# A post-norm attention and mixture-of-experts layer on eight cores: the softmax bound's broadcast moved behind the first score matmuls

## The reference, cut to what matters

```python
def reference(x, Wq, bq, Wk, bk, Wv, bv, Wo, bo, Wg, W1, W2, W3, bias):
    # x: (4, 2048, 2048); 16 heads of 128; 8 experts, 2 per token, FFN 1024
    q, k, v = proj(Wq, bq), proj(Wk, bk), proj(Wv, bv)
    q, k = apply_rotary(q), apply_rotary(k)
    attn = softmax(q @ k.T * 128 ** -0.5)
    a = (attn @ v) @ Wo.T + bo
    x = layernorm(x + a)
    w = top2(sigmoid(x @ Wg.T) + bias)
    f = sum over e of (silu(x @ W1[e].T) * (x @ W3[e].T) * w[e]) @ W2[e].T
    return layernorm(x + f)
```

## Time and profile before

| | us |
|---|---|
| median of 3 runs | 3051.35 |
| lowest and highest run | 3049.73, 3329.33 |
| the profiled execution | 3052.92 |
| its span (first to last instruction, slowest core, core 6) | 3051.4 |
| spans of the eight cores | 3035.5 to 3051.4 |
| PE busy | 2589.0 |
| DVE busy | 772.0 |
| ACT busy | 593.5 |

### The profile page before, as it was taken

How to read it: one execution, slowest core, us unless ns; L and a number is a source line. 1 busy time by engine, 2 the same in 40 slices (tenths; PEclk the granted TensorE clock), 3 DMA queues, 4 the chain that set the end, 5 groups by cost and what they waited for, 6 DMA issues and landing times.

```text
span 3051.4 us, 31195 instructions; the slowest of 8 cores (3035.5 to 3051.4 us)
## 1 busy us (share of the span) xinstructions
PE 2589.0 (85%) x12262; PEld 1193.6 (39%) x12262; DVE 772.0 (25%) x1140; ACT 593.5 (19%) x761; POOL 172.5 (6%) x323
## 2 busy tenths in 40 slices
PE   4778788888887878799579998999999899998993
PEld 3234343435352525244134343444434344343441
DVE  0222222222213131321632213122221312212126
ACT  0342424242423333342100000000000000000031
POOL 1000000000000000000000001010010100001000
PEclk9889999899898999999589999999999999999996
DMA  9310101010101010024134444443444434344423
GB/s 147 49 28 14 28 14 28 14 28 15 28 14 28 15 28 8 7 36 76 26 51 73 62 79 65 70 76 64 79 65 77 65 67 76 63 76 63 69 45 121
DMA packets 50720, 155.26 MB, mean 51 GB/s; under 512 B 6162, under 2 KB 6290, under 8 KB 49298
## 3 DMA queue, kind: packets, MB, share of 16 engines
q0 software_dynamic: 47264, 142.69, 28.8%
q1 hardware_dynamic: 3314, 10.59, 1.0%
HBM read 287.54 MB, written 8.39 MB: 97 GB/s over the span
## 4 chain that ended last, share of the span: by engine, by line
PE 74%; DMA 9%; DVE 8%; issue 5%; ACT 3%; DVEq 0%; ACTq 0%; POOL 0%; POOLq 0%
PE pb L776 15%; PE pb L793 14%; PE pb L850 9%; DMA wslab<-w_t 7%; PE pb L318 6%; PE pb L395 6%; PE pb L401 6%; PE pb L448 4%; PE pb L468 4%; PE pb L539 4%; PE pb L454 3%; DMA R_bf<-x_t 2%; DVE scr_f L341 1%; ACT scr_bf L361 1%; PE pb L370 1%
## 5 line engine op out<-in xcount | busy, mean ns | idle before, releaser
L850 PE MATMUL pb<-aog,wslab 128*128 128x512 bf16 x2048 | 460.6, 381 | 61.6 <-DMA wslab<-w_t 60.9
L776 PE MATMUL pb<-xy,wslab 128*128 128x512 bf16 x2048 | 464.4, 386 | 0.0
L793 PE MATMUL pb<-xy,wslab 128*128 128x512 bf16 x2048 | 452.5, 379 | 0.0
L787 ACT ACTIVATE scr_bf<-pb 128x512 bf16<-128x512 f32 x128 | 69.5, 594 | 1326.9 <-PE pb L776 1326.9
L850 PEld LDWEIGHTS pb<-aog,wslab 128*128 128x128 bf16 x2048 | 195.3, 98 | 323.4 <-issue 102.8
L476 ACT ACTIVATE scr_bf<-pb,mq_sb 128x1024 bf16<-128x1024 f32 x256 | 285.1, 1114 | 136.0 <-PE pb L468 135.9
L395 PE MATMUL pb<-R_bf,wslab 128*128 128x512 bf16 x768 | 297.4, 387 | 5.8 <-ACT vbuf L306 5.8
L776 PEld LDWEIGHTS pb<-xy,wslab 128*128 128x128 bf16 x2048 | 202.4, 99 | 251.5 <-issue 18.8
L401 PE MATMUL pb<-R_bf,wslab 128*128 128x512 bf16 x768 | 296.4, 386 | 0.0
L793 PEld LDWEIGHTS pb<-xy,wslab 128*128 128x128 bf16 x2048 | 200.3, 98 | 241.7
L863 DVE TENSOR_TENSOR R_f<-pb,R_f 128x512 f32<-128x512 f32 x256 | 177.1, 692 | 347.4 <-PE pb L850 334.1
(11 more groups left out here) (111 smaller groups left out, 1460.6 us busy)
## 6 DMA issues: line engine op xcount, KB each, us to landing
wslab<-w_t POOLq DMA_DIRECT2D x128, 512.0 KB, 5.1
wslab<-w_t POOLq DMA_DIRECT2D x128, 256.0 KB, 3.8
wslab<-wv_t POOLq DMA_DIRECT2D x8, 1024.0 KB, 8.5
R_bf<-x_t POOLq DMA_DIRECT2D x16, 512.0 KB, 7.3
wslab<-wq_t POOLq DMA_DIRECT2D x8, 1024.0 KB, 8.5
wslab<-wk_t POOLq DMA_DIRECT2D x8, 1024.0 KB, 8.0
wslab<-wo_t POOLq DMA_DIRECT2D x16, 512.0 KB, 5.0
y<-R_f SPq DMA_DIRECT2D x16, 512.0 KB, 2.7
```

Of the source, the lines that this page charges most:

```text
L776: last = t.matmul(pa[nc2].ap(), wslab.ap()[:, W1OFF[s1] + dc * 128: W1OFF[s1] + dc * 128 + 128], xy.ap()[:, dc * TL + nc2 * 512: dc * TL + ...
L793: last = t.matmul(pa[4 + nc2].ap(), wslab.ap()[:, W3OFF[s1] + dc * 128: W3OFF[s1] + dc * 128 + 128], xy.ap()[:, dc * TL + nc2 * 512: dc * ...
L850: last = t.matmul(pa[wb + nc2].ap(), wslab.ap()[:, W2OFF[s2] + fc * 128: W2OFF[s2] + fc * 128 + 128], aog.ap()[:, fc * TL + nc2 * 512: fc ...
```

## The change

The broadcast of the bound (the matmul and the write of `mq_sb`) leaves `bound_finale` and becomes a function of its own, `bound_bcast`. It uses bank pa6 in place of pa3. `st_merged` now issues the scores of chunks 0 and 1, then this function, then both exps, then the sums of chunk 0; from chunk 2 on the loop is as it was: scores, exp, sums of the chunk before.

```diff
--- before.py
+++ after.py
@@ -429,18 +429,20 @@
                 A(lambda s: s.activation(msc.ap()[0:1, 7:8], msc.ap()[0:1, 7:8],
                                          AF.Exp, scale=0.5),
                   r=["msc"], w=["msc"])
+
+            def bound_bcast():
                 T(lambda t: t.matmul(
-                    pa[3].ap()[:, 0:1], ones_r_f.ap(), msc.ap()[0:1, 7:8],
-                    start=True, stop=True), r=["msc", "ones"], w=["pa3"])
+                    pa[6].ap()[:, 0:1], ones_r_f.ap(), msc.ap()[0:1, 7:8],
+                    start=True, stop=True), r=["msc", "ones"], w=["pa6"])
                 V(lambda v: v.tensor_scalar(
-                    mq_sb.ap()[:, 6:7], pa[3].ap()[:, 0:1], -1.0, None,
-                    ALU.mult), r=["pa3"], w=["mq"])
+                    mq_sb.ap()[:, 6:7], pa[6].ap()[:, 0:1], -1.0, None,
+                    ALU.mult), r=["pa6"], w=["mq"])
 
             proj_rope(4, 4096 + hl * 2048, ["ws2" if hl == 0 else "ws3"], bkc,
                       "bkc", ck_sb, sk_sb, kbuf, koff,
                       [f"kb{hl}_{i}" for i in range(4)], finale=bound_finale)
 
-            def st_merged():
+            def st_merged(pre=None):
                 def sums_pvs(kc):
                     j = kc % 2
                     so = (1 - j) * 1024
@@ -461,7 +463,7 @@
                             r=[f"sb{2 * (1 - j) + qb}", f"vb{kc}"],
                             w=[f"pa{4 + qb}"])
 
-                for kc in range(NDC):
+                def emit_mms(kc):
                     j = kc % 2
                     for qb in range(2):
                         T(lambda t, kc=kc, j=j, qb=qb, qoff=qoff, koff=koff:
@@ -472,6 +474,9 @@
                             start=True, stop=True),
                             r=[f"kb{hl}_{kc // 4}", f"qb{hl}_{qb}"],
                             w=[f"pa{2 * j + qb}"])
+
+                def emit_exp(kc):
+                    j = kc % 2
                     so = (1 - j) * 1024
                     A(lambda s, j=j, so=so: s.activation(
                         scr_bf.ap()[:, so:so + 1024],
@@ -479,8 +484,18 @@
                         scale=SCALE),
                         r=[f"pa{2 * j}", f"pa{2 * j + 1}", "mq"],
                         w=[f"sb{2 * (1 - j)}", f"sb{2 * (1 - j) + 1}"])
-                    if kc >= 1:
-                        sums_pvs(kc - 1)
+
+                emit_mms(0)
+                emit_mms(1)
+                if pre is not None:
+                    pre()
+                emit_exp(0)
+                emit_exp(1)
+                sums_pvs(0)
+                for kc in range(2, NDC):
+                    emit_mms(kc)
+                    emit_exp(kc)
+                    sums_pvs(kc - 1)
                 sums_pvs(NDC - 1)
 
             def epilogue_m():
@@ -503,7 +518,7 @@
                         AF.Identity, bias=bvc.ap()[:, hh:hh + 1]),
                         r=[f"ao{hh}", "bvc"], w=[f"ao{hh}"])
 
-            st_merged()
+            st_merged(pre=bound_bcast)
             epilogue_m()
 
     for gi in range(NH // 2):
```

## The result

The changed kernel took 3069.62 us (median of 10 runs) against 3049.64 us for the kernel before (median of 10 runs on the same chip): the ratio is 1.0067, with a 95% interval of 1.0056 to 1.0078. It is slower by 20 us, 0.7%. In some executions of both kernels (near 3400 us), and in the profiles of x3, x4 and x11 further down, the cores of a die ran at a lower granted clock than the others, and the ratios and the means over cores leave them out.

The account below looks back on a forecast made before the run. The prediction took PE's matmul stream as the bound. A later first exp (11.2 us) and a later clock return (17.6 us) summed to 28.8 us, giving a forecast of 3080 us, range 3060 to 3096.

Parts of the forecast that it names:

- What bounds the kernel: TensorE's matmul stream, busy 85% of the span; the step from key projection to attention loop comes once in 16 heads.
- What the change removes: On PE, L336 and the scores of chunk 0 no longer stand behind the 2.56 us wait, finishing before anything needs them.
- What it adds: On DVE, mq waits behind L341, L345 and L349, so first exp and sums come 0.70 us later per head: 11.2 us.
- The loop edit: Two score steps issued ahead of the attention loop cost and give nothing, since PE and ACT keep their order.
- The flush on DVE: A flush behind L349 by the skill page, 0.96 us per head, 15 us in all; left out of the sum.
- The clock: PE's clock returns 3.1 us later, 2.4 us more at half clock, at 0.46 per us: 1.1 per head, 17.6 us.
- list of signs: What the new trace would show if right or wrong; mq starting before L349 ends on DVE counted as wrong.
- Sum: Whole kernel: 11.2 + 17.6 = 28.8 us slower, 3080 us, 0.9% more; under 2% not told from no change.
- Shift alone: Rival: PE's clock return moves with the work, so only 11.2 us are added, 3063 us; chance 0.17.
- Not slower: Rival: unbroken PE work ahead of the sums brings the clock back early, -3 us in all, 3048 us; chance 0.08.
- Half clock through the loop: Rival: the pause keeps PE's clock down through the whole attention loop, 264 us more, 3315 us; chance 0.03.
- A deeper prefetch: Rival: the loop keeps scores one chunk further ahead, removing waits before the exps, 72 us less, 2979 us; chance 0.01.

Follow-up runs that it names:

- x3: Changed kernel with mq written ahead of L349 on DVE, not behind it, PE's order unchanged; ratio 1.0066 to the kernel before.
- x4: Changed kernel with 8 unneeded matmuls per head, 3 ahead of the scores of chunk 1, 5 ahead of the sums; ratio 0.9960 to the kernel before, median 3032.16 us.
- x11: Changed kernel with 9 unneeded matmuls in each of two PE pauses between the heads; ratio 1.0038 to the kernel before.
- x6: x4 with 11 in place of 5 matmuls ahead of the sums, and L349 done twice for the last key pair; ratio 1.0048 to the kernel before, 3062.33 us.
- x1: Changed kernel with broadcast and mq write put back in their old place, only the loop edit kept; ratio 1.0020 to the kernel before, median 3050.87 us.
- x2: Changed kernel with mq written between L341 and L345, broadcast ahead of the scores of chunk 1; ratio 0.9920 to the kernel before, median 3016.27 us.
- x7: x2 with 3 unneeded matmuls per head, 2 ahead of the broadcast, 1 ahead of the sums; ratio 0.9873 to the kernel before, median 3010.38 us.
- x8: x7 with 18 more unneeded matmuls per head ahead of the second L370 of the keys; ratio 0.9858 to the kernel before, median 3010.13 us.
- x9: x8 with 9 unneeded matmuls ahead of the first L370 of the query projection and of the first key half; ratio 0.9833 to the kernel before, 3002.56 us.
- x5: Kernel before the change with 5 unneeded matmuls per head between L370 and the broadcast L432; ratio 0.9991 to the kernel before, median 3048.38 us.

## Why the prediction was right, point by point

- *What bounds the kernel* stood. PE's stream is what counts, and the step comes 16 times in the same form.
- *What the change removes*: the wait of L432 is gone and L336 follows L370 at once, and this gained nothing by itself, as said.
- *What it adds*: DVE decides and not PE, as said. The first exp was forecast at 4.28 to 4.44 and measured at 4.20, the sums at 5.67 and measured at 5.57. The term of 0.70 us per head was 0.60: L341 began at 0.36, not at 0.41 or later, since it overlaps the end of L423, as L437 overlaps the end of L349. The first exp came only 0.51 later; the rest of the 0.60 is that the sums now start 1.37 us behind it, where I took the 1.28 of before. That was 9.6 us in place of 11.2. x6 shows, in the filled kernel, that the term is carried to the end in full.
- *The loop edit* does nothing, as said (x1).
- *The flush on DVE*: L437 begins 0.07 us before the recorded end of L349, and the repeated addition in x6 cost 1.31 us for an operation of 1.23. The 0.96 us that an estimate from the Trainium skill ("VectorE: DVE Perf Modes", "The DRAIN you can't avoid") would put behind each isn't there. The prediction told that section in part: it also says that a next operation that is not held starts earlier, and the trace agrees with that. The prediction's own list of signs called it wrong if mq starts before L349 ends; by 0.07 us it does, as the prediction's steps for mq themselves allow, so that sign was badly put.
- *The clock* was the right mechanism and the largest term. Its return was forecast 3.1 us later, 2.4 of them in the loop, at 0.46 us each: 17.6 us. Measured were 2.06 us more in the loop, and 13 us are left for them. So the shift was a little high, and the upper bound of 3.8 was not reached. The price of 0.46 us lies between two measures of it. The pairs of kernels whose sums start at the same place give 0.47 to 0.49 (1.79 us for 3.84 from the changed kernel to x4, 1.22 for 2.50 from x2 to x7, 0.55 for 1.12 from x8 to x9); the comparison with the kernel before gives 0.40. It was read from two heads that differ in the loop, and I used it for shifts of the whole step; here it was right since the later return lies in the loop, and in x5 it was wrong for what lies ahead of it. Luck has a part: the 3.1 us were the spread between two kinds of heads of the kernel before, chosen between two bounds, and nothing in the rows tied them to the new pauses.
- *Sum*: 28.8 forecast (3080, range 3060 to 3096), 22.9 in the step and 20 in all (3069.62). The last exp of a head was forecast 1.8 us later and came 1.43 later. 2 us were given back between the heads, which the prediction had not looked at. That nothing under 2% tells itself from no change was too strong: the interval of the ratio lies well above 1, and even above the 0.2% of x1.
- *Shift alone* (3063) fell: half clock in the loop grew by 2.06 us, and the last exp moved by 1.43 where the sums moved by 0.60.
- *Not slower* fell: no early return lasted. Its reasoning was half right: in 26 of the 128 heads of the eight cores the clock was back early, like the first head of core 7 above, and in each of them it fell again ahead of the sums and came back for good at 10.5 us or later. With both pauses filled, in x4, it lasted: 0.04 us of half clock are left in a loop.
- *Half clock through the loop* fell: by the exp of chunk 4 the clock was up in every head. Near the start of the loop in x5, though, it fell again behind two pauses of 0.42 and 1.05 us. The page "TensorE: Matmul & The Clock Gate" of the Trainium skill describes, under "A second HAM failure mode: psum-queue depth-cycling", short idles between groups of matmuls that make the clock swing between its levels. The x5 rows look like that; no run here shows that it is the same cause.
- *A deeper prefetch* fell: the order inside the loop is that of before, and x1 gained nothing.

What stays open: why the same pauses between the heads bring the clock down in some heads and not in others. In x3 and x7 the work between the heads is that of their neighbours and only its place in time differs, so that place is the likely reason; it was not varied by itself, and by what rule it would act no run shows.

## What to carry to other kernels

When an operation is moved off one engine's critical path, read where it lands in the queue of the engine that finishes it: here a write of 0.16 us went behind 3.7 us of work on DVE, and everything waited for it. The same broadcast with its write two operations further ahead gains 24 us where the change lost 20. And a pause of PE is worth two looks, once for its length, and once for the clock afterwards in the stretch where PE is the one waited for; matmuls that compute nothing can pay there. They did where both pauses of the step were filled (x4, 33 us), and gave nothing where one of two was (x5).

## What the runs showed that I had not expected

- Half clock can come back elsewhere: taken out of the step it came back between the heads (x7: 42 us less of it in A, 30 us more in B), and taken out between the heads some came back in the step (x9). Over half of such a gain can be lost. It need not be: in x4 120 us of it went out of A, and B had 10 us less too.
- Two kernels with one and the same stream of instructions measured 0.2% apart, with an interval that leaves out 1 (1.0008 to 1.0032), and the eight cores of one profile spanned 3015 to 3053 us. Between the cores of that profile the half clock differs with the span; that this pattern also makes the 0.2% was not tested.
- Five matmuls of filling (2.1 us) in PE's pause (x5) brought the clock back at 0.8 us in the head shown, and it was lost again at 4.2 us, for 3.4 us: an early return is not kept by itself.
